# Second feed-forward of a two-layer gated transformer: from all-experts dense to sorted rows for 24 of 32 token tiles

## The reference, cut to what matters

```
xt = layernorm(x)                                   # (4096, 256)
logits = tanh(xt @ Wg1.T) @ Wg2.T                   # (4096, 8)
top_logits, top_idx = top_k(logits, 2);  scores = softmax(top_logits)
up   = einsum('td,ehd->teh', xt, Wup) + bup         # 8 experts, 128 hidden each
down = einsum('teh,eoh->teo', silu(up), Wdown) + bdown
x = x + tanh(g_ffn[1]) * sum over the two chosen e of scores[e] * down[e]
```

## Time and profile before

| what | us |
|---|---|
| median of three runs | 1808.64 |
| profiled execution, its own time | 1795.94 |
| span of it, first to last instruction | 1794.1 |
| PE busy (matmul) | 1619.7 |
| DVE busy | 1160.6 |
| ACT busy | 738.2 |
| POOL busy | 423.3 |
| mean granted TensorE clock | 0.971 |

### The profile page before, as it was taken

One profiled execution on the slowest core, in us unless ns is written; L12 is line 12 of the kernel. 1 busy time (PEld: TensorE's weight loads), 2 busy tenths in 40 slices (PEclk: granted clock), 3 DMA queues, 4 the chain that ended last, 5 costly groups with the idle time before them and its releaser, 6 DMA issues.

```text
span 1794.1 us, 42480 instructions
## 1 busy us (share of the span) xinstructions
PE 1619.7 (90%) x14740; PEld 1361.1 (76%) x14740; DVE 1160.6 (65%) x3029; ACT 738.2 (41%) x1508; POOL 423.3 (24%) x464
## 2 busy tenths in 40 slices
PE   3899999978998899998799999999999997799998
PEld 2566666656776689997688888888888886578887
DVE  5888888886567655456466666666666654465655
ACT  2466666652322225554333333333333332344443
POOL 3555555522224210000222111221221111000000
PEclk8999999999999999999899999999999998799999
DMA  7566666642101015433200000000000000000000
GB/s 203 114 126 126 124 125 126 125 74 67 38 30 42 24 42 156 143 124 111 77 27 22 20 26 21 20 23 27 20 26 20 21 15 6 1 24 12 12 24 24
DMA packets 127357, 107.07 MB, mean 60 GB/s; under 512 B 10442, under 2 KB 120195, under 8 KB 127020
## 3 DMA queue, kind: packets, MB, share of 16 engines
q1 hardware_dynamic: 121068, 89.07, 21.2%
q0 software_dynamic: 6208, 16.95, 2.9%
HBM read 49.22 MB, written 56.77 MB: 59 GB/s over the span
## 4 chain that ended last, share of the span: by engine, by line
PE 53%; DVE 24%; issue 10%; ACT 6%; SPq 3%; DVEq 1%; DMA 1%; ACTq 1%
PE bank L544 10%; PE bank L546 9%; PE bank L545 9%; PE bank L1020 4%; PE bank L606 3%; PE bank L615 2%; PE bank L1048 2%; PE bank L629 2%; PE bank L570 2%; DVE rm_b L2281 2%; PE bank L646 2%; DVE rs_b L2289 2%; DVE probs_b L2284 1%; DVE oT_b_lo L2273 1%; PE bank L633 1%
## 5 line engine op out<-in xcount | busy, mean ns | idle before, releaser
L544 PE MATMUL bank<-xT_b_hi,m_hi 128*128 128x256 f32 x512 | 154.1, 301 | 23.9 <-ACT qT L1390 12.0
L1411 ACT ACTIVATE probs_b<-probs_b 128x512 f32<-128x512 f32 x64 | 40.4, 632 | 324.9 <-DVE probs_b L2284 324.9
L1584 POOL TENSOR_TENSOR probs_b<-probs_b,rs_b 128x512 f32<-128x512 f32 x64 | 66.8, 1043 | 454.0 <-DVE rs_b L2294 453.7
L544 PE MATMUL bank<-n_hi,oT_b_hi 128*128 128x256 f32 x512 | 149.7, 292 | 5.8 <-DVE x L2252 5.8
L545 PE MATMUL bank<-xT_b_hi,m_lo 128*128 128x256 f32 x512 | 145.8, 285 | 0.0
L546 PE MATMUL bank<-xT_b_lo,m_hi 128*128 128x256 f32 x512 | 145.7, 285 | 0.0
L545 PE MATMUL bank<-n_hi,oT_b_lo 128*128 128x256 f32 x512 | 145.1, 283 | 0.0
L546 PE MATMUL bank<-n_lo,oT_b_hi 128*128 128x256 f32 x512 | 145.0, 283 | 0.0
L1194 ACT ACTIVATE probs_a<-probs_a 128x512 f32<-128x512 f32 x128 | 80.4, 628 | 114.4 <-DVE probs_a L1723 114.0
L1020 PEld LDWEIGHTS bank<-ctxT_b,qT 128*128 128x128 f32 x1024 | 125.2, 193 | 2.7
L544 PEld LDWEIGHTS bank<-xT_b_hi,m_hi 128*128 128x128 f32 x512 | 98.9, 193 | 30.5 <-ACT qT L1390 15.0
(11 more groups left out here) (316 smaller groups left out, 4786.7 us busy)
## 6 DMA issues: line engine op xcount, KB each, us to landing
sorted_x<-zeros SPq DMA_DIRECT2D x16, 2112.0 KB, 14.7
xg<-sorted_x SPq DMA_DIRECT2D x71, 128.0 KB, 2.1
sorted_y<-ys SPq DMA_DIRECT2D x71, 128.0 KB, 2.0
w_raw<-in_w SPq DMA_DIRECT2D x16, 408.0 KB, 3.8
x<-in_x SPq DMA_DIRECT2D x4, 1024.0 KB, 7.1
cx_raw<-in_ctx SPq DMA_DIRECT2D x32, 128.0 KB, 2.6
out<-x SPq DMA_DIRECT2D x8, 512.0 KB, 2.9
ctxT_a<-in_ctxT SPq DMA_DIRECT2D x16, 128.0 KB, 2.2
```

Source lines behind the costliest of these rows:

```text
L544: pe.matmul(dst, lh, rh, start=start, stop=False, skip_group_check=True)
L1584: pool.tensor_tensor(probs_b[b], probs_b[b], rs_b[:, b, :].unsqueeze(2).broadcast_to([P, G1, S]), ALU.mult).then_inc(s["b_probs"], 1)
```

## The change

The second feed-forward's 32 tiles are divided. Tiles 24 to 31 go through the dense blocks as before (2 blocks instead of 8). Tiles 0 to 23 are sent to their two experts alone.

- Rounds 2 to 13 of the second attention (12 rounds) each route the two tiles that round i - 1 finished: norm at the end of the DVE round before (`norm_f`), 4 transposes on PE right after the first scores (`turn_f`), 6 logit matmuls (`logits_f`), a tanh on ACT (`tanh_f`), two small matmuls (`back_f`), top two and counts on DVE (`largest_f`, `counts_f`), two small matmuls for the places (`place_f`), slots on DVE (`slots_f`), and 4 indirect DMAs on POOL (`scatter_f`). `rsqrt` works on 4 columns instead of 2. The loop is unrolled by two.
- Round 14 makes the table (31 tiles of 256 rows: expert and first row of each) and the places. The split of the dense weights moves from all rounds into round 15, as 8 pieces of 512 columns.
- A new stage of 31 row tiles of 256 rows follows, then the two dense blocks. While the dense blocks run, POOL gathers the results of 24 tiles (48 indirect DMAs, three buffers), and DVE adds them: 9 tiles in the first block, 15 in the second.
- Square root and router split are gone from the transition; the router is split in round 1 and the bias in the new stage.

```diff
+R1 = 2 * P
+NJ1 = TOP * FIRST_DENSE * P // R1 + E - 1          # 31
+NX1, NH1, NY1, NG1 = 3, 3, 3, 3
# SP
+            sp.wait_ge(s["b_resid"], START + NA * 2)
+            sp.dma_start(bd1..., a["bdown"][0:E, :]...broadcast_to([P, E * D])).then_inc(s["w1_loaded"], 16)
+            for j in range(NJ1 + 2):
+                if j + NX1 - 1 < NJ1:
+                    load_rows1(j + NX1 - 1)
+                if j >= 2:
+                    store_rows1(j - 2)
# load_rows1(j): waits x_xT_psum of tile j - 3, value_load of the row, dma_start of 256 rows
# store_rows1(j): waits x_y_ready of tile j, dma_start of 256 rows
# PE, a round
                 scores1(i, 0, ...)
+                if route is not None:
+                    turn_f(i, route)               # waits g_xn_ready, that is norm_f
                 rest(outputs1, 3)
...
# PE, new stage
+            for j in range(NJ1 + 2):
+                if j + 1 < NJ1:
+                    turn_x2(j + 1)                 # waits x{j % 3}_loaded; 4 transposes
+                if j < NJ1:
+                    up_x2(j)                       # 6 matmuls of 256 columns
+                expert_f(j + 1)                    # value_load
+                if j >= 2:
+                    down_x2(j - 2)                 # 6 matmuls of 256 columns
# ACT, new stage
+            for j in range(NJ1):
+                if j + 1 < NJ1:
+                    xh_x2(j + 1)                   # copy of 128x512
+                silu_x2(j)                         # value_load, two Silu of 128x256
# POOL: stage(j): value_load, two tensor_copy of 128x256 (one expert's up weights)
# DVE, new stage
+            for j in range(NJ1 + 2):
+                if j + 1 < NJ1:
+                    xl_x2(j + 1)                   # 128x512
+                if j < NJ1:
+                    hl_x2(j)                       # 128x256
+                if j >= 2:
+                    y_x2(j - 2)                    # value_load, 128x512
+                if j == 2:
+                    rsqrt(rstd[...], nmr[...], 8, NT - FIRST_DENSE, ...)
+                if j == 12:
+                    split_bias()
+                if j == 20:
+                    norm(0, 0)
# DVE, a round's end
                     add_tile(i * 2 + 5)
                     stats_b(i + 2)
+                    if not first:
+                        norm_f(i - 1, ...)
# DVE, dense blocks
+                    if i == 0 and t >= 1:
+                        add_f(t - 1)
+                    if i == 1:
+                        add_f(9 + t + t // 2)
+                        if t % 2 == 1:
+                            add_f(10 + t + t // 2)
# POOL, dense blocks: gather_f(tile) waits for the add of tile - 3, then two indirect DMAs
```

More of the change, by code:

```diff
@@ L67, in rounds, with rounds_b @@
     body(n - 1, last=True)
-def pairs(eng, n, body):
-    with eng.Fori(0, n // 2 - 1) as j:
+def rounds_b(eng, body):
+    body(0, first=True)
+    body(1)
+    with eng.Fori(1, NR // 2 + 1) as j:
         for u in range(2):
-            body(j * 2 + u, u, True)
-    body(n - 2, 0, True)
-    body(n - 1, 1, False)
+            body(j * 2 + u, route=u)
+    body(NA - 2, late=True)
+    body(NA - 1, last=True)
 class Steps:
@@ L701, in _ @@
             pe.sem_inc(s["a_loop_done"], 1)
[L703 to L713, removed]
-                    else:
[L715 to L723, removed]
+            ph, f, chunks, hidden = "f1", f1, NC1, HID1
@@ L770, in down_part @@
[L770 to L803, removed]
-                            if t == at["weights"]:
-                                turn_weights(i + 1, 1 - u)
-                        if 0 <= t - 3 < chunks:
-                            down_part(i, u, t - 3)
@@ L1120, in _ @@
+            turn(0, 0, 1)
+            logits(0, 0)
+            logits_back(0, 0)
+            turn_weights(0, 0)
+            for i in range(BLOCKS1):
+                block_(i, i % 2, i + 1 < BLOCKS1)
+            pe.wait_ge(s[f"{ph}_resid"], START + BLOCKS1)
         @block.scalar
@@ L1413, in next_q @@
                 def next_q(*cs):
-                    if not last:
+                    if last:
+                        for c in cs:
+                            w1_high(c)
+                    else:
                         for c in cs:
@@ L1420, in attend1 @@
                     oth(i - 1, 3)
+                if route is not None:
+                    xh_f(i)
+                if late:
+                    act.wait_ge(s["g_counted"], NF + NR)
+                    act.activation(dl1, dl1, ACT.Tanh, scale=0.5).then_inc(s["g_exp_ready"], 1)
                 expo(1)
@@ L1952, in ffn @@
-                norm(0, 0)
-                xT_low(0, 0, 0)
-                xT_low(0, 0, 1)
-                largest(0, 0)
-                weights(0, 0)
-                weights_low(0, 0)
-                with ve.Fori(0, NF // 2 - 1) as j:
-                    st.loop(j, STEPS[ph])
-                    for u in range(2):
-                        block_(j * 2 + u, u, True)
-                st.end(NF // 2 - 1)
-                block_(NF - 2, 0, True)
-                block_(NF - 1, 1, False)
+                    other = f["s"][c % 2]
@@ L2278, in centre, with attend1 @@
+            def attend1(i, first=False, route=None, late=False, last=False):
+                more = not late and not last
                 def centre(b):
@@ L2311, in attend1 @@
                     xT_low1(i + 1)
+                if not first and route is None and more:
+                    setup_f()
+                if route is not None:
+                    largest_f(i)
+                    counts_f(i)
                 centre(3)
@@ L2338, in _ @@
             attend1(0, first=True)
-            with ve.Fori(1, NA - 2) as i:
-                st.loop(i, STEPS["b"], 1)
-                attend1(i)
-            st.end(NA - 2)
-            attend1(NA - 2, more=False)
-            attend1(NA - 1, more=False, last=True)
+            attend1(1)
+            with ve.Fori(1, NR // 2 + 1) as j:
+                st.loop(j, STEPS["b"], 1)
+                for u in range(2):
+                    attend1(j * 2 + u, route=u)
+            st.end(NR // 2 + 1)
+            attend1(NA - 2, late=True)
+            attend1(NA - 1, last=True)
             otl(NA - 1, 3)
@@ L2357, in _layouts @@
+            xT_low(0, 0, 0)
+            xT_low(0, 0, 1)
+            largest(0, 0)
+            weights(0, 0)
+            weights_low(0, 0)
+            for i in range(BLOCKS1):
+                block_(i, i % 2, i + 1 < BLOCKS1)
+            st.wait()
 def _layouts(v):
```

950 lines of the change are left out of this document (673 added, 277 removed).

## The result

The changed kernel took 1831.82 us in the median (1830.14 to 1832.22, four runs) beside 1809.15 for the kernel before (1806.33 to 1812.31): ratio 1.0123, 95% interval 1.0105 to 1.0141. It is slower by 22.7 us, 1.2%; 1783.0 had been predicted.

The account below looks back on a forecast made before the run. PE was taken to set the pace in the attention and dense blocks. Removed blocks -186.4, rounds +41, new stage +122, transition -11, last block +8.7 gave -25.7 us: 1783 us, own range 1758 to 1806, 8 in 10 from 1737 to 1812.

Parts of the forecast that it names:

- PE held up by DVE's `norm_f` at the turn: Head of each routed attention round: PE waits 2.5 us for the norm, last in DVE's round.
- (C): Rival, attention rounds: Tanh between Exps makes ACT reload tables, 31 us more at worst, 1814 us; chance 4%.
- the six blocks removed: Second feed-forward: six dense blocks fall away, -186.4 us.
- the transition: Between attention and feed-forward: work moves into the new stage, block 0's routing stays at 13.3 us; -11 us.
- the chain of the new stage: Each load waits behind an earlier tile's store: two tiles per 7.0 us, 3.5 a tile at full clock.
- twelve rounds and their tail: Second attention: 3.3 us more a round, 40 us over 12 rounds; attention ends 41 us later.
- new stage: 31 row tiles: 122 us, at 3.75 a tile, the middle between full clock (3.5) and lower clock (4.05).
- last block: Last dense block: POOL's gathers at 2.54 us a tile limit it, 39.3 us against 30.6, +8.7.
- first block beyond 33.4: First dense block: its 9 adds, 9 us on DVE, fit beside DVE's other work.
- (B): Rival: the gap at each round's head drops PE's clock, 41 us over 12 rounds, 1824 us; chance 13%.
- the 3.3 of the sum: Growth taken for each routed round: waiting, turn, logits and small matmuls, less waits PE has anyway; 3.3 us.
- "swallowed": Attention rounds: later waits that PE has anyway absorb some 0.7 us of the delay at the round's head.

Follow-up runs that it names:

- the loop written out: The changed kernel with VectorE's loop over the twelve routed rounds written out, no branch: 1803.95 us, ratio 1.0052 to the kernel before.
- the filling: The changed kernel plus 10 unneeded matmuls ahead of turn_f's wait and 5 ahead of each new-stage turn from the third tile: 1794.96 us, ratio 1.0005.
- the kernel at 41.47: The changed kernel with turn_f later, a fourth buffer for the new stage's gathered rows and VectorE's loop written out: 1719.83 us, ratio 0.9591.
- a filled one: Round of the changed kernel with VectorE's loop written out and 10 unneeded matmuls ahead of turn_f's wait, new stage unfilled: 1802.55 us, ratio 0.9967.
- the fastest version: The changed kernel with late turn_f, fourth buffer, VectorE's loop written out, adds shared 12 and 12, store three behind: 1708.37 us, ratio 0.9528 to the kernel before.

## Why the prediction was wrong

Right: PE held up by DVE's `norm_f` at the turn, 2.34 us a round; Tanh without a table load, so that (C) fell; the six blocks removed; the transition, 14.1 us from PE's first transposes against 13.3; store, load and landing as the chain of the new stage. ScalarE ran ten Tanhs of 0.36 us among the Exps and no load from 1000 to 1440. The Trainium skill (ScalarE: Activation LUTs, section Table sets) has exp and tanh in one set, and this case agrees.

Wrong, by steps of the sum, for the first comparison, with the borders of the stages as in the rows above:

| step | predicted | measured | miss |
|---|---|---|---|
| twelve rounds and their tail | +41 | +66.8 | 25.8 |
| new stage | +122 | +132.7 | 10.7 |
| last block | +8.7 | +16.3 | 7.6 |
| first block beyond 33.4 | 0 | +2.7 | 2.7 |
| transition | -11 | -10.1 | 0.9 |

Together 47.7: from -25.7 to +22.0.

*The rounds* are the largest miss, as large as the whole gain that had been forecast. The step that failed is that the sum has no term for TensorE's clock: I gave it to a rival, (B), with 13%. I had its row, a gap of 2.4 us followed by the lower level, and argued that dense work on both sides would keep the clock up. It doesn't: every wait of 2.34 us at the turn, and every one of 1.97 with the loop written out, came with a dip, while waits of up to 0.87 us in the kernels without such a wait came with none.

The runs split the 5.7 us: from 40.29 to 41.47 is the added work, 1.18; to 43.56 the wait, 2.09; to 45.25 TensorE's clock, 1.69; to 45.97 DVE's loop, 0.7. The order in which the edits are made shifts this a little: with the loop left as it was, the filling gained 1.56. And the filling is somewhat longer than the 1.97 us that PE waited in that kernel, so 1.69 is rather too low for the clock. Work and wait make 3.27, the 3.3 of the sum, and that is not luck: in the kernel at 41.47 PE is busy 2.1 us a round more than before and idle 0.9 less, where the sum has 1.6 of work and 0.7 "swallowed".

(B)'s price was too high, 3.4 a round against 1.69, since it took every dip as 6.8 us long, and in the runs behind the 1.69 only one in four is. A round with the short dip took 1.3 us more than a filled one, with the long dip 2.7. But (B)'s own threshold, a round longer by 5.4, was passed. 12 x 1.69 = 20 us, of the 25.7 that the change should have won. With these 20 in it the sum would have come to -5 and not to +22.0: the other terms did the rest.

DVE's loop was not among the steps at all. The change doubles its body; I priced the instructions added and not the going around. It took another 9 us here, in two ways: PE waits 2.34 us at the turn and not 1.97, and the dip is the long one in every second round and not in every fourth.

*The new stage*: the mechanism was right. The term from the transposes to the store was 4.3 us in the mean instead of 3.5, and 3.9 where the clock was up; the landing took 2.7 instead of 2.4. I had 4.05 a tile for the chain at the lower level and took the middle, 3.75; it was 4.19. How much of the 10.7 us is the clock's stays open, since the filled stage tells little.

*The last block*: 42.4 us in the profile without a stall, 39.3 forecast, and the terms listed for it add up to 38.3 only. I had twelve tiles' gathers left at its start, at 2.54 us each. Without a stall GpSimd's last 32 gathers start from 1757.0 to 1798.6, 1.34 us apart, and the block begins at 1764.9: thirteen tiles of 2.68 us are left, 34.8 us instead of 30.5. 4.5 us more in the first comparison are the stall's. No step allowed for it.

My range ended at 1812, where most of (B) began.

What stays open: why long bursts of indirect DMAs stop ScalarE and VectorE in some sets and not in others; and what holds a tile of the fastest version at 2.54 us, where the engines' sum was 2.1.

## What to carry to other kernels

A wait that a change puts ahead of dense TensorE work costs its length and then the dip behind it (here 2.0 to 2.3 us of waiting and 1.7 of clock); price both, and ask first whether the waiting instruction can stand behind other work. A row that shows such a dip after a gap of that length outweighs an argument why this gap should differ. Look at the going around of a loop when its body grows. And where one engine issues loads and stores in turn, look at which store each load stands behind: here one place later was worth 2%.

## What was unexpected of the hardware

- DVE stood 3.1 to 3.9 us at its loop's head once the body was two rounds, with one fetch of 8 KB within each stand, and 28 or 29 from 960 to 1440 instead of 2; with one round a body it never did.
- Under 16 scatters issued back to back (20 us) ScalarE stood up to 19.9 us, marked "remote", where it otherwise waits 8.2 for PE; under 20 gathers it stood 10.5 and VectorE 6.3. This came in two of the five sets and in the first comparison only. Under 8 scatters in the same sets such waits of ScalarE were 3.7 us or less. Breaking the burst of 16 took the loss away (ratio 0.994).
- Ten matmuls of 512 columns that nobody needed, put into a wait of 2 us in twelve rounds, took 1.56 to 1.69 us off each round, about 1% of the kernel, since the clock stayed up.
